# A two-layer gated cross-attention block with routed experts: the order of second attention, fourth norm and router rewoven

## The reference

```
x = x + tanh(g_xattn[0]) * attention(layernorm(x), ctx)      # 32 heads, rotary, mask
x = x + tanh(g_ffn[0])   * linear(layernorm(x))              # dequantised, masked weight
x = x + tanh(g_xattn[1]) * softmax(Q K^T * scale) @ ctx      # one head of 512, Q = norm(x) Wq + bq
x = x + tanh(g_ffn[1])   * experts(layernorm(x))             # 32 experts, the best 2 of each token
```

## Time and profile before

| | |
|---|---|
| time, median of 3 | 898.61 us (898.56 to 899.48) |
| profiled execution | 893.93 us, span 892.0 us, mean granted clock 0.972 |
| PE / DVE / ACT / POOL busy | 93% / 73% / 45% / 49% of the span |
| chain that ended last | PE 79%, DVE 8%, POOL 5%, DMA 4%, ACT 2% |

### The profile page before, as it was taken

One profiled execution on the slowest core, in us unless ns is written; L12 is line 12 of the kernel. 1 busy time (PEld: TensorE's weight loads), 2 busy tenths in 40 slices (PEclk: granted clock), 3 DMA queues, 4 the chain that ended last, 5 costly groups with the idle time before them and its releaser, 6 DMA issues.

```text
span 892.0 us, 13114 instructions
## 1 busy us (share of the span) xinstructions
PE 832.7 (93%) x4337; PEld 695.5 (78%) x4337; DVE 654.5 (73%) x1299; ACT 397.7 (45%) x1009; POOL 437.0 (49%) x386
## 2 busy tenths in 40 slices
PE   5878999999999999999999999999999999999980
PEld 4766888888888888888888888878878687877860
DVE  3775778876778886677886778876853568998875
ACT  4633434434324433433432433445224447987970
POOL 5488537634635833634753553540020058888840
PEclk9999999999999999999999999999999979999995
DMA  8402101100210200120110020020224517999717
GB/s 329 171 1 95 71 1 47 71 2 1 80 39 1 103 15 0 47 71 1 59 59 0 26 115 1 4 92 18 95 94 155 213 71 259 345 344 379 284 44 284
DMA packets 23641, 91.13 MB, mean 102 GB/s; under 512 B 6576, under 2 KB 7088, under 8 KB 15776
## 3 DMA queue, kind: packets, MB, share of 16 engines
q1 hardware_dynamic: 17440, 81.00, 24.8%
q0 software_dynamic: 6144, 9.46, 3.0%
HBM read 86.23 MB, written 14.68 MB: 113 GB/s over the span
## 4 chain that ended last, share of the span: by engine, by line
PE 79%; DVE 8%; POOL 5%; DMA 4%; ACT 2%; issue 1%; SPq 1%; POOLq 0%; ACTq 0%; DVEq 0%
PE bank L145 22%; PE bank L147 21%; PE bank L146 21%; PE bank L1716 6%; PE bank L1723 3%; DVE cT_lo L1231 3%; DMA last_xn<-xn_rows,place_token 2%; DVE x L1489 1%; PE bank L139 1%; DMA raw_v<-in_wv 1%; PE bank L1529 1%; PE bank L1564 1%; DVE xT_lo L1225 1%; PE bank L1623 1%; POOL qT L584 1%
## 5 line engine op out<-in xcount | busy, mean ns | idle before, releaser
L584 POOL TENSOR_TENSOR qT<-straight,turned 128x512 f32<-128x512 f32 x64 | 82.7, 1293 | 147.2 <-DVE turned L1278 147.0
L888 ACT ACTIVATE probs<-bank,negmax 128x128 f32<-128x128 f32 x256 | 90.7, 366 | 128.6 <-DVE negmax L1289 128.6
L1278 DVE TENSOR_TENSOR turned<-bank,sinT 64x512 f32<-64x512 f32 x160 | 110.2, 689 | 2.2
L145 PE MATMUL bank<-xT_hi,wq_hi 128*128 128x512 f32 x256 | 105.7, 413 | 1.0 <-POOL wq_lo L563 1.0
L145 PE MATMUL bank<-wo_hi,oT_hi 128*128 128x512 f32 x256 | 100.8, 394 | 1.9 <-POOL wo_lo L571 1.8
L146 PE MATMUL bank<-xT_lo,wq_hi 128*128 128x512 f32 x256 | 101.5, 397 | 0.0
L147 PE MATMUL bank<-xT_hi,wq_lo 128*128 128x512 f32 x256 | 101.3, 396 | 0.0
L147 PE MATMUL bank<-wo_hi,oT_lo 128*128 128x512 f32 x256 | 100.5, 393 | 0.0
L146 PE MATMUL bank<-wo_lo,oT_hi 128*128 128x512 f32 x256 | 100.3, 392 | 0.0
L895 ACT ACTIVATE pT_hi<-bank 128x512 fp32r<-128x512 f32 x64 | 38.3, 598 | 133.1 <-PE bank L1723 133.0
L1231 DVE TENSOR_TENSOR cT_lo<-ring,cT_hi 128x1024 fp32r<-128x1024 f32 x72 | 88.7, 1233 | 9.3 <-ACT cT_hi L811 9.2
(11 more groups left out here) (225 smaller groups left out, 2045.1 us busy)
## 6 DMA issues: line engine op xcount, KB each, us to landing
ring<-in_ew SPq DMA_DIRECT2D x36, 1024.0 KB, 8.4
raw_big<-in_wq SPq DMA_DIRECT2D x9, 1024.0 KB, 4.8
raw_big<-in_wo SPq DMA_DIRECT2D x8, 1024.0 KB, 4.8
ring<-picked SPq DMA_DIRECT2D x8, 512.0 KB, 7.7
raw_k<-in_wk SPq DMA_DIRECT2D x8, 256.0 KB, 5.0
ctx_raw<-in_ctxT SPq DMA_DIRECT2D x4, 512.0 KB, 6.0
raw_v<-in_wv SPq DMA_DIRECT2D x8, 256.0 KB, 4.9
x<-in_x SPq DMA_DIRECT2D x2, 1024.0 KB, 11.7
```

The source lines that it names most:

```text
L145: nc.tensor.matmul(out_, hi, r_hi, start=start, stop=False)
L584: nc.gpsimd.tensor_tensor(dst, straight[:, k, :], turned[:, k, :], ALU.add).then_inc(rope_sum, 1)
L888: ex = nc.scalar.activation(probs[:, u % 2, h, :], bank_scores[u % 2][:, h * S:(h + 1) * S], ACT.Exp, bias=negmax[:, u % UNITS, h:h + 1], ...
L1278: last = nc.vector.tensor_tensor(turned[dst, k, :], bank[src, :], sinT[src, tok], ALU.mult)
```

## The change

Nothing of what is computed changes. The order of calls changes on three engines, from item 12 of the projection to the last `codes`:

- TensorE: `turn_probs1(0)` and the four products of `attend1(0, ...)` go in between items 12, 13, 14 and 15. `router_turn` and `logits` of tiles 0 and 1, then of 2 and 3, go ahead of and in between the parts of the second half's attention. The three short fills (4, 2 and 3 products) go; the last one (16) stays. The order of `rank`, `codes`, `router_turn` and `logits` for tiles 3 to 7 is new.
- ScalarE: `router_std(0)` and `router_norm(0)` to `(3)` go ahead of `exps1(1)`. Two small activations on a new tile `warm` (one Exp, one Sqrt, each of one column) are added around it.
- VectorE: `attended(0)` to `(3)`, `normed(0)`, `choose(0)`, `choose(1)`, `find_place(0)` and `choose(2)` go ahead of `attended(4)`.
- Banks: tiles 0 to 5 share banks 0 and 1, tiles 6 and 7 have 4 and 5. `router_turn(2)` to `(5)` therefore wait for `choose` of the tile two before (`r_best`).

```
@@ -153,6 +153,7 @@
         scale2 = sb("scale2", [P, KC])
         eps = sb("eps", [P, 1])
         shift = sb("shift", [P, NB])
+        warm = sb("warm", [P, 2])
         f_words, f_small, f_float, f_deq = (sem(f"f_{n}") for n in ("words", "small", "float", "deq"))
         w_parked = nc.dram_tensor("w_parked", [P, KC, E], F32, kind="Internal").ap()
         HALF = T // 2
@@ -392,7 +393,7 @@
             return psum[(7, 4)[t % 2]]
 
         def router_bank(t):
-            return psum[(0, 1, 4, 5)[t % 4]]
+            return psum[(0, 1, 0, 1, 0, 1, 4, 5)[t]]
 
         def result(lane):
             return loaded[:, lane, :] if lane < LANES // 2 else late_results[:, lane - LANES // 2, :]
@@ -1009,31 +1010,31 @@
                 keep(11)
                 exps1(0)
                 keep(12)
+                probs_kept(0)
                 keep(13)
-                probs_kept(0)
-                keep(14)
-                keep(15)
                 act.wait_ge(f_small, 16 * 9)
                 nc.scalar.activation(before[:, :], before_raw[:, :], ACT.Copy).then_inc(exact, 1)
                 act.wait_ge(constants, 1)
                 nc.scalar.activation(ones[:, :], ones_raw[:, :], ACT.Copy).then_inc(exact, 1)
                 nc.scalar.activation(eb3[:, :], eb_raw[:, :], ACT.Copy).then_inc(exact, 1)
+                keep(14)
+                router_std(0)
+                keep(15)
+                for t in range(4):
+                    router_norm(t)
+                nc.scalar.activation(warm[:, 0:1], eps[:, :], ACT.Exp)
+                router_kept(0)
+                router_kept(1)
                 exps1(1)
+                nc.scalar.activation(warm[:, 1:2], eps[:, :], ACT.Sqrt)
+                router_kept(2)
                 probs_kept(1)
-                router_std(0)
-                router_norm(0)
-                router_norm(1)
-                router_kept(0)
+                router_kept(3)
                 router_std(1)
-                router_norm(2)
-                router_kept(1)
-                router_norm(3)
-                router_kept(2)
                 router_norm(4)
-                router_kept(3)
-                router_std(2)
                 router_norm(5)
                 router_kept(4)
+                router_std(2)
                 router_norm(6)
                 router_kept(5)
                 router_norm(7)
@@ -1427,28 +1428,33 @@
                 softmax_shift(0)
                 softmax_scale(0)
                 dve.wait_ge(m_in, 48)
-                attended(0)
-                attended(1)
+                for t in range(4):
+                    attended(t)
+                normed(0)
                 softmax_shift(1)
-                attended(2)
-                attended(3)
+                choose(0)
+                choose(1)
                 softmax_scale(1)
+                find_place(0)
+                choose(2)
                 attended(4)
-                normed(0)
                 attended(5)
+                find_place(1)
+                choose(3)
+                normed(1)
                 attended(6)
-                choose(0)
-                normed(1)
-                choose(1)
-                find_place(0)
                 attended(7)
-                choose(2)
+                find_place(2)
                 normed(2)
-                find_place(1)
-                for t in range(3, NB):
-                    choose(t)
-                    find_place(t - 1)
-                find_place(NB - 1)
+                find_place(3)
+                choose(4)
+                choose(5)
+                find_place(4)
+                choose(6)
+                find_place(5)
+                choose(7)
+                find_place(6)
+                find_place(7)
                 weight_diff()
                 dve.wait_ge(r_codes, NB)
                 write_rows(slice(0, NX), psum[3][:, 0:NX], 0)
@@ -1548,11 +1554,12 @@
 
                 def router_turn(t):
                     pe.wait_ge(ln_norm, 3 * NB + t + 1)
-                    if t < 4:
-                        pe.wait_ge(ln_lo, 3 * NB)
+                    if t < 2:
+                        pe.wait_ge(g_kept, 4 * KC)
+                    elif t < 6:
+                        pe.wait_ge(r_best, 2 * t - 2)
+                    else:
                         pe.wait_ge(g_pkept, 2)
-                    else:
-                        pe.wait_ge(r_best, 2 * t - 6)
                     for c in range(KC):
                         mm = nc.tensor.transpose(router_bank(t)[:, c * P:(c + 1) * P], last_xn[:, t, c * P:(c + 1) * P], ident[:, :])
                     mm.then_inc(r_turned, 1)
@@ -1831,37 +1838,50 @@
                 project1(11)
                 score1(0)
                 project1(12)
+                turn_probs1(0)
                 project1(13)
-                turn_probs1(0)
+                attend1(0, range(2))
                 project1(14)
+                attend1(0, range(2, 4))
                 project1(15)
-                attend1(0, range(2))
                 score1(1)
-                attend1(0, range(2, 4))
-                pe.wait_ge(constants, 2)
-                pe.wait_ge(ln_lo, 3 * NB)
-                fill(0, 4)
-                turn_probs1(1)
-                fill(0, 2)
-                attend1(1, range(4))
-                fill(0, 3)
                 router_turn(0)
                 router_turn(1)
                 logits(0)
                 router_turn(2)
                 logits(1)
+                turn_probs1(1)
+                pe.wait_ge(constants, 2)
+                pe.wait_ge(ln_lo, 3 * NB)
                 rank(0)
                 router_turn(3)
-                for t in range(2, NB):
-                    logits(t)
-                    if t + 2 < NB:
-                        router_turn(t + 2)
-                    rank(t - 1)
-                    codes(t - 2)
-                pe.wait_ge(g_added, NB)
-                rank(NB - 1)
-                codes(NB - 2)
-                codes(NB - 1)
+                logits(2)
+                attend1(1, range(2))
+                rank(1)
+                codes(0)
+                logits(3)
+                attend1(1, range(2, 4))
+                rank(2)
+                codes(1)
+                rank(3)
+                codes(2)
+                router_turn(4)
+                router_turn(5)
+                logits(4)
+                codes(3)
+                router_turn(6)
+                logits(5)
+                rank(4)
+                router_turn(7)
+                logits(6)
+                rank(5)
+                codes(4)
+                logits(7)
+                rank(6)
+                codes(5)
+                rank(7)
+                codes(6)
+                codes(7)
                 count_all()
                 fill(6, 16)
                 turn(0)
```

## The result

The median after is 904.68 us (902.52 to 907.11, 8 runs) against 896.72 us (892.41 to 899.48, 8 runs) before: ratio 1.0089, with an interval of 1.0069 to 1.0109. That is 8 us slower, where 7.7 was forecast, and inside the range given. Single executions of one kernel differ by several microseconds here; the profiled one after (907.11 us, span 905.1) is the longest of its eight, so the stage is compared by its own length and not by the spans.

What follows compares the result with a forecast made beforehand. It took the chain through the slot table to GpSimd's gathers as the bound. The table's +7.75 us took the profiled 893.93 to 901.7; for the median, 898.61 + 7.7 = 906.3 us, range 900.4 to 910.6.

Steps and rivals of the forecast that it cites:

- `score1(1)` 2.8 later behind `keep(15)`: First half: with four tiles of attention and `keep(15)` behind `router_std(0)` in front, `score1(1)` starts 2.8 us later.
- The warm loads: ScalarE, middle: each table switch for `warm` costs 1.28 us, without the 1.38 us drain the Trainium skill adds.
- `attended(7)` at 39.07: End of the middle: VectorE finishes the last tile's attention at 720.1, 2.3 us later than before.
- Four waits in the tail: TensorE's tail: `rank(3)`, `codes(2)`, late `router_std(2)` and `codes(3)` hold up ready work; table at 740.65, +7.75 us.
- the walk: Call-by-call timing of the tail at half-clock prices, from `codes(2)` at 721.9 to the slot table at 740.65.
- The clock at half from 720: Tail: with TensorE all but empty from 716 to 722, half the clock from 720 until the sixteen fills.
- The rival with the clock up: Tail at full clock: table at 736.0, +3.1 us, 901.7 us; chance 0.12.
- The early fall: Rival: the clock falls already near 709, `attended(7)` at 723.5 instead of 720.1; +11.1 us, 909.7 us; chance 0.15.
- The three short fills that go cost nothing: TensorE: removing three short fills, nine products in gaps, adds no time.
- One for one to the end: Expert stage: nothing in it waits for a fixed time, so a shift of the slot table reaches the end whole.
- The rival that is faster: Tail: the four waits in TensorE's list fall away; table at 727, -5.8 us, 892.8 us; chance 0.08.

Runs made afterwards that it cites:

- e4: Kernel before the change, with only the first half's attention taken in between items 12 to 15 and the router as before: +2.7 us (1.3 to 5.2).
- e10: The kernel of e6 without the two `warm` activations: stage 54.91 us against 54.84, `attended(7)` at 39.30 against 39.21.
- e5: Changed kernel with only TensorE's list reordered, `rank(3)`, `codes(2)` and `codes(3)` moved to where their operands are ready: ratio to before 1.0028.
- e3: Changed kernel with GpSimd's `mark_place(3)` ahead of `code(4)` instead of behind it: ratio to before 1.0081.
- e2: Changed kernel with ScalarE's `router_std(2)` ahead of `router_kept(4)` instead of behind it: ratio to before 1.0104.
- e1: Changed kernel with 33 extra products, results unread, where TensorE stands empty in its tail: ratio to before 1.0050.
- e6: Changed kernel with the fills of e1 and 12 more in the middle, where TensorE waits earlier: stage 54.84 us, +3.5 us by the runs.
- e9: Changed kernel with the list of e5, the middle fills of e6 and 7 more fills ahead of `router_turn(4)` and `rank(3)`: ratio to before 0.9991.
- e7: Kernel before, reordered so all eight tiles' attention precedes nearly all of the router, with late `codes`: 889.90 us, ratio to before 0.9918.

## Why the prediction was right, step by step

- *`score1(1)` 2.8 later behind `keep(15)`*: right in size, 2.68 after and 2.76 at `attended(7)` in e4, where the first half was changed alone. One part of its account was wrong: `router_std(0)` ahead of `keep(15)` cost nothing. The idle ahead of `score1(1)` is 0.78 after, 0.78 in e4 without that call, and 0.78 ahead of `score1(0)` before. It is the time of `keep` itself (0.69), which before ran under the two tiles of `attend1` behind item 15 and now has nothing to run under.
- *The warm loads*: right. The load at 704.60 lasts 1.28 and the next activation follows at 705.89. The Trainium skill (ScalarE: Activation LUTs, "What ACT_TABLE_LOAD costs") states about 1.38 us of drain beside each load; no run here shows it (0.01 us in e10), and the measurement decides.
- *`attended(7)` at 39.07*: right at 38.91, in an execution whose clock held to 721.
- *Four waits in the tail*: three of four. `rank(3)`, `codes(2)` and `codes(3)` start within 0.3 us of the walk once the later start of the stage (1.1 us) is taken off (predicted 720.35, 721.9, 728.7; 721.19, 722.72, 729.54 measured). Mending the three took 6.4 us off the tail (e5), `codes(3)` alone 2.3 (e3). `router_std(2)` was late as forecast, and its lateness cost nothing (e2): `router_turn(6)`, which needs it, stood behind `codes(3)` anyway. I had not asked which of the two waits ended last.
- *The clock at half from 720*: right (0.64 in the microsecond from 721). Its price is 4.5 us (e1), against 4.65 between the forecast and the rival in which the clock stays up (740.65 less 736.0).
- *The rival with the clock up* gave +3.1; e6, which made it so, has +3.0 by the stage and +3.5 by the runs.
- *The early fall*: the mis-sized one. Chance 0.15; it came in four of the five profiles that have the change's middle without fills there (e1, e2, e3, e5, not after). Price 3.4 up to `attended(7)`; measured 2.2 to 2.6, since the clock is back at 1.00 by 717 to 720. Such a stage (e2, with the tail as after) is 10.0 us over before, where I wrote 11.1. How many of the eight timed executions after had it isn't known. So there is luck in how near 7.7 and 8.0 lie: the profile after is the one in five without the early fall, and e2, the same order but for a call that cost nothing, measured +10.0 (the intervals of the two overlap).
- *"The three short fills that go cost nothing"*: this step most likely failed. I looked only at the gaps that they fill. In e6, e9 and e10, with twelve fills back in the middle (three more than went, at other places), the clock was 1.00 there and `attended(7)` lay at 39.2 to 39.3; without them it lay at 41.1 to 41.5 in four of five profiles. Three against five executions make this likely and do not prove it. In the profile after it happened not to matter.
- *One for one to the end*: right by the medians (stage +7.4, time +8.0).
- *The rival that is faster* asked that the waits fall away. e5 and e9 took them away and were not faster: the late second half (2.4 us at full clock: 39.2 for 36.77) stayed. e7 has neither the waits nor the late second half, and is faster.

## What to carry to other kernels

In a list that an engine takes in order, put each call where its operands will be there, and read every wait by what stands ready behind it: moving three calls took 6.4 us off the tail, while an early norm behind such a wait was worth nothing. Weaving an early half's next step into a late half delayed the late half here by 2.4 us at full clock, and that half was the path: ask first what the last tile pays. A fill that looks idle may hold the clock for the products around it (likely here, not proven); take it out only with the granted clock of that stretch in view.

## What the runs showed of the hardware

The same order of products on TensorE had its clock at 1.00 from 708 to 720 in one profile (after) and at 0.50 for six whole microseconds of that stretch in four others, with the waits ahead of it alike (0.34 and 0.68 us at 706.87 and 708.60 after, 0.34 and 0.69 in e2). TensorE was not idle when it fell, and just as busy where it held: in e1 it shows 2.97 of the 4 us from 708 as busy, and after, at the same place in the order (the 4 us from 706.14, as its stage begins 1.86 us sooner), 2.98. What decides it stays open. The fills that went with a held clock closed gaps and added wide products at once, so the runs do not tell the two apart.
